# Degrees from a summed one-hot, two more groups multiplied in layer 0, fewer split feature sets: a two-layer graph kernel on one core

## What is computed

```python
deg = segment_sum(ones, dst); iso = deg == 0
def layer(h, edge_feats, Wn, Ws, Wi):
    msg = (h[src] + edge_feats) @ Wn.T
    agg = segment_sum(msg, dst) / maximum(deg, 1)[:, None]
    x = agg + where(iso[:, None], h @ Wi.T, h @ Ws.T)
    return where(x >= 0, x, SLOPE * x)
h = layer(x, edge_attr, Wn0, Ws0, Wi0)
h = layer(h, edge_attr, Wn1, Ws1, Wi1)
return layernorm(x + h)
```

## Time and profile before

| what | us |
|---|---|
| median of 3 runs | 1078.83 (1078.09 to 1083.72) |
| the profiled execution, its own time | 1072.14 |
| its span, first to last instruction | 1070.3 |
| windows of layer 0 on PE, about | 39 to 640 |
| windows of layer 1 on PE, about | 680 to 1058 |

### The profile page before, as it was taken

The page is one execution under the profiler, slowest core; times in us unless marked ns, Lnnn a source line. Parts: engine busy times, 40 slices in busy tenths (PEclk is TensorE's granted clock), DMA queues, the critical chain, the costliest instruction groups (busy, mean ns, idle before and its releaser), DMA issues.

```text
span 1070.3 us, 38440 instructions
## 1 busy us (share of the span) xinstructions
PE 942.5 (88%) x14592; PEld 880.3 (82%) x14592; DVE 696.6 (65%) x2388; ACT 534.1 (50%) x1143; POOL 756.2 (71%) x757
## 2 busy tenths in 40 slices
PE   1599899989899798998979987989899989999994
PEld 0499888978799687888878877989889989999994
DVE  8868776876778767887677782355455545554334
ACT  7456565655566555765656661353245525533200
POOL 8367767777777777777777671777767767767671
PEclk9999999999999989999999977999999999999998
DMA  9467777877788758877877777767656856676772
GB/s 306 158 214 248 256 252 240 264 259 233 244 283 277 255 169 268 285 241 255 261 220 230 242 243 241 238 172 218 177 157 171 236 157 168 170 222 168 206 217 60
DMA packets 141368, 237.75 MB, mean 222 GB/s; under 512 B 20050, under 2 KB 101308, under 8 KB 138620
## 3 DMA queue, kind: packets, MB, share of 16 engines
q1 hardware_dynamic: 80832, 144.35, 41.2%
q0 software_dynamic: 35584, 72.92, 25.1%
q10 hardware_dynamic: 24764, 17.95, 5.4%
HBM read 182.71 MB, written 52.43 MB: 220 GB/s over the span
## 4 chain that ended last, share of the span: by engine, by line
PE 45%; POOL 8%; issue 6%; DVE 4%; DMA 3%; ACT 3%; ACTq 2%; SPq 1%; DVEq 0%; POOLq 0%
PE ps_dense L1341 16%; PE ps_count L1341 11%; POOL rows L577 8%; PE ps_count L1329 6%; PE ps_win L1280 6%; PE ps_self L1399 3%; DMA rows<-x_parts_rows,idx 2%; ACT counts L1127 2%; PE ps_node L1412 2%; DMA h_parts<-h_parts_rows 1%; DVE h_rest L926 1%; SPq L498 1%; ACTq L1102 1%; PE ps_win L1287 1%; PE ps_count L1333 1%
## 5 line engine op out<-in xcount | busy, mean ns | idle before, releaser
L1127 ACT CAST counts<-ps_count 128x294 f32 x992 | 456.8, 502 | 346.0 <-PE ps_count L1329 207.4
L577 POOL DMA_INDIRECT rows<-x_parts_rows,idx x442 | 446.8, 1011 | 158.1 <-issue 125.0
L1341 PE MATMUL ps_dense<-counts,h_parts 128*128 128x136 bf16 x5292 | 450.3, 226 | 11.4 <-DVE sums L825 7.2
L1341 PEld LDWEIGHTS ps_dense<-counts,h_parts 128*128 128x128 bf16 x5292 | 350.6, 99 | 44.8 <-issue 9.2
L577 POOL DMA_INDIRECT rows<-h_parts_rows,idx x286 | 279.3, 977 | 127.6 <-issue 86.0
L1329 PE MATMUL ps_count<-is_code,is_lane 128*128 128x294 bf16 x992 | 285.5, 312 | 31.9 <-ACT counts L1127 27.2
L1280 PE MATMUL ps_win<-onehot,feats 128*128 128x40 f32 (+1 forms) x1564 | 253.4, 241 | 33.7 <-DMA rows<-x_parts_rows,idx 13.3
L1280 PEld LDWEIGHTS ps_win<-onehot,feats 128*128 128x128 f32 (+1 forms) x1564 | 212.7, 163 | 40.1 <-issue 25.5
L790 DVE TENSOR_SCALAR is_lane<-column,lane 128x128 bf16<-128x128 bf16 x496 | 138.4, 279 | 99.9 <-PE ps_count L1333 91.4
L792 DVE TENSOR_SCALAR is_code<-codes,code 128x637 bf16<-128x637 f16 x496 | 198.6, 400 | 0.0
L1280 PE MATMUL ps_win<-onehot,rows 128*128 128x40 bf16 (+1 forms) x2224 | 150.4, 187 | 2.3 <-DVE sums L803 2.3
(11 more groups left out here) (99 smaller groups left out, 790.6 us busy)
## 6 DMA issues: line engine op xcount, KB each, us to landing
feats<-in_edges_dram SPq DMA_DIRECT2D x196, 256.0 KB
counts_kept<-counts SPq DMA_DIRECT2D x20, 1764.0 KB
counts<-counts_kept SPq DMA_DIRECT2D x140, 252.0 KB
rows<-x_parts_rows,idx POOLq DMA_INDIRECT x442
x_parts_rows<-h_parts SPq DMA_DIRECT2D x7, 672.0 KB, 8.0
h_parts<-h_parts_rows SPq DMA_DIRECT2D x7, 672.0 KB, 8.7
h_parts_rows<-row_parts ACTq DMA_DIRECT2D x16, 288.0 KB
rows<-h_parts_rows,idx POOLq DMA_INDIRECT x286
```

The costliest lines, as they stand in the source:

```text
L577: nc.gpsimd.indirect_dma_start(rows[:, SUB * slot + c, :], None, table[:, :], bass.IndirectOffsetOnAxis(ap=indices[:, c:c + 1], axis=0)).t ...
L1127: nc.scalar.copy(counts[:, buffer_of(j), :, at(offset + first, count)], ps_count[:, COUNT_BANK[q], 0:count * TILES].rearrange("p (r t) -> ...
L1341: last = nc.tensor.matmul(bank, h_parts[:, t, k, :], counts[:, b, t, 0:WIDE], start=(t == 0 and k == 0), stop=(t == TILES - 1 and k == PAR ...
```

## The change

1. DVE gets one more step a window in layer 0, `sum_hot`: a reduction that adds the four one-hots (128x4x40, f32) to `hot_sum` (128x40). PE then makes one product with the ones instead of four. The step waits for the one-hot that it adds; PE waits for its result ahead of the last product of the window.
2. USED takes in groups 13 and 37: 22 groups are multiplied in layer 0, at 6.2 tiles a beat. LATE has 9 left. Eight windows are no longer gathered in layer 0. The number of builds (31 groups) and of groups multiplied in layer 1 stays; two groups are built in layer 0 and not in layer 1.
3. SPLIT_RATE is 0.3: 58 windows are split and not 78.

The beats of both layers stay 202 and 77.

```diff
-    USED = sorted([g for g in KEPT if g % 3 == 0] + [7, 19, 31, 43])
+    USED = sorted([g for g in KEPT if g % 3 == 0] + [7, 13, 19, 31, 37, 43])
-    BUILDS, MULTIPLIED, BUILT_BEAT, DONE_BEAT = plan_layer0(len(USED), 176, BUFFERS, GC, TILES, 5.6, 8)
+    BUILDS, MULTIPLIED, BUILT_BEAT, DONE_BEAT = plan_layer0(len(USED), 176, BUFFERS, GC, TILES, 6.2, 8)
-    SPLIT_RATE = 0.4
+    SPLIT_RATE = 0.3
+        hot_sum = sb("hot_sum", [P, HOT, W])
+            def sum_hot(n):
+                h = SUB * (n % HOT)
+                dve.wait_ge(onehot_ready, n + 1)
+                nc.vector.tensor_reduce(hot_sum[:, n % HOT, :],
+                                        onehot[:, h:h + SUB, :].rearrange("p c w -> p w c"),
+                                        AX.X, ALU.add).then_inc(hot_summed, 1)
                 for n in range(HOT):
                     make_onehot(n)
+                for n in range(HOT):
+                    sum_hot(n)
...
                     if k + 2 in SPLIT_OF:
                         split_feats(k + 2)
+                    if 1 <= k and k - 1 + HOT < WINDOWS:
+                        sum_hot(k - 1 + HOT)
...
                     if layer == 0:
-                        last = sum_degrees(ps_win[n % 2], onehot[:, SUB * (n % HOT):SUB * (n % HOT + 1), :], W, c + 1)
+                        pe.wait_ge(hot_summed, n + 1)
+                        last = nc.tensor.matmul(ps_win[n % 2][:, 0, DEG * W:(DEG + 1) * W], ones16[:, :],
+                                                upper(hot_sum[:, n % HOT, :]), start=True, stop=True)
                     last.then_inc(window_summed, 1)
```

More of the change, by code:

```diff
@@ L315, in gnn_resnorm_kernel @@
         onehot_ready = sem("onehot_ready")
+        hot_summed = sem("hot_summed")
         rows_gathered = [sem(f"rows_gathered{j}") for j in range(ROWS)]
```

## The result

The changed kernel takes 1083.79 us (median of 11 runs, 1079.75 to 1092.87) against 1078.09 us for the kernel before on the same chip (11 runs, 1073.14 to 1083.72). The ratio is 1.0054, 95% interval 1.0027 to 1.0080: slower by 5.7 us, where 1076 us was forecast, 3 us less than before.

A forecast was written before the change was run, and what follows sets the result against it. POOL and PE were taken as almost level in layer 0, PE as the bound of layer 1. Layer 0 at +5 and layer 1 at -6.6 us made -2, rounded to -3: 1076 us, range 1060 to 1094 (the forecast's own 1066 to 1084).

The forecast's parts named there:

- "up to 10 us" for fewer splits: POOL, layer 0: 20 fewer splits, less contention with DVE's subtractions, give POOL up to 10 us on top of 41.
- The prices on PE: PE, layer 0: prices per product, chunk and build taken from distances of starts; they sum to +18.9 us.
- the -6.6 forecast: Layer 1: PE loses 9.6 us of builds, one more restart waiting for ACT costs 3 us; -6.6 us.
- The load of the reduction: DVE, layer 0: 196 reductions at 0.33 us each, priced from two in setup, 65 us more on DVE.
- the 3 us in the sum for what DVE does late: Layer 0: PE's added waits for DVE's late adds of windows and groups, net of fewer last products; +3 us.
- 13.3 us of waits for rows: PE, layer 0: its waits for POOL's rows vanish because POOL has 41 us less work; -13.3 us.
- 5 us of clock: Layer 0: part of the lower granted clock comes back as the waits for rows go; about -5 us.
- Rival B: Layer 0, beats with a register load: DVE becomes the bound and its stops reach PE; +17, 1093 us; chance 0.24.
- Rival C: Layer 0: PE runs clean once rows are early, idle 36 us, half the clock loss back; 1062 us; chance 0.22.
- the terms of the sum: Both layers: PE's added products and builds against waits for rows, clock and layer 1; +9 us for parts 2 and 3.

The follow-up runs named there:

- no_deg_one: Kernel before with 22 groups and 58 splits, no reduction, and one column number loaded per beat instead of seven every seventh: 1049.89 us, ratio 0.9758.
- before_one: Kernel before with one column number loaded to a register in each beat instead of seven in every seventh: 1071.06 us, ratio 0.9957.
- all_but_deg: Kernel before with 22 groups and 58 splits but without the reduction (four products of degrees stay on PE): 1075.67 us, ratio 0.9991.
- deg_only_one: Kernel before with only the reduction added (20 groups, 78 splits) and one column number loaded per beat: 1080.93 us, ratio 1.0036.
- after_one: Changed kernel with one column number loaded in each beat of layer 0 instead of seven in every seventh: 1053.29 us, ratio 0.9788.
- pairs_one: Changed kernel with one addition in pairs and two products replacing the reduction and one product, and one column number loaded per beat: 1051.26 us, ratio 0.9750.
- after_early: Changed kernel with the load of seven column numbers moved to the end of the beat before: 1092.28 us, ratio 1.0128.

## Why the prediction was wrong

**POOL, right.** POOL was the bound of layer 0 and left it: PE's waits for rows went from 13.3 to 3.0 us, POOL's for PE from 20 to 79. `no_deg_one` against `before_one` shows that parts 2 and 3 are worth 21 us once PE can use the room. The "up to 10 us" for fewer splits was high: in the trace of before a gather that overlapped a subtraction took 1.07 us on average and another 0.98, about 3 us for 20 splits. That the reduction takes nothing from POOL holds: after the change, gathers beside it took 0.99 us and gathers beside neither 1.00.

**The prices on PE, right to within some 5 us.** PE's busy time in layer 0 rose by 20 us for 18.9 counted, but part of the rise is the lower clock of that one trace.

**Layer 1, right.** From its first to its last add of a window it is 371 us and was 379, for the -6.6 forecast. No waits for loads of counts came up.

**The load of the reduction, a size.** 0.33 us was taken from reductions of another shape; 0.43 us was measured, near the upper bound given. That is 19 us more on DVE. With its stops DVE was 91% taken (505 busy and 45 stopped of 605 us), for 90% forecast.

**The step that failed** is the 3 us in the sum for what DVE does late, and with it the two gains that it left standing in full, 13.3 us of waits for rows and 5 us of clock. PE's waits for the adds of windows rose by 10.0 us and those for groups by 0.8, 10.8 us and not 3. They took the place of the 10.3 us of waits for rows that went: PE's idle time stayed at 54 us, and the clock, which was to rise with less idling, did not (0.956 over the runs). The forecast was 8.7 us below the median of the change (-3 against +5.7); the waits are 8 us of it and the clock 5, and terms that came out better, layer 1 for one, give some back.

The mechanism behind the 3 us was wrong too. They were sized as half of PE's waits for adds and a tenth of those for groups, as if lateness grew with the load of DVE. `all_but_deg` has no reduction, and PE waits for the adds as long as in the changed kernel. What reaches PE in these two kernels is the single long load. (Load alone can make the adds late too: `deg_only_one` has no long load, and PE waits 13.2 us for them.) The rows held the warning: 28.2 us in 18 stops, the longest 4.6 us, was read as an average of 1.6 us. With two banks at about three us a beat, loads of up to 2.5 us never reached PE in the changed kernel and those of 3.2 us and more always did. `after_one` shows the size: taking away the long loads, with more time spent on loads in all, is worth 30 us with the reduction, 26 without (`all_but_deg` to `no_deg_one`), and 6 with 20 groups and no reduction.

**Rival B** named the right place, the beats with a register load, with a chance of 0.24, and the right sign; the 1093 that it gave was too high. Its account was not right: it made the reduction the cause, by the slack that it takes from DVE, and that slack (77.5 us in `all_but_deg`, 32 in the changed kernel) made no difference to the waits for adds. **Rival C**, PE running clean once rows are early, is what was left when the long loads went: in `after_one` PE is idle 36 us in layer 0, as C had it, at a clock of 0.97, and the time is 1053 for its 1062.

For parts 2 and 3 alone the terms of the sum give 33.6 - 13.3 - 5 - 6.6 = +9 us. They measured nothing with loads of seven and -21 us with single ones. In the second pair idle time fell by 24 us (49 to 25) and the clock in layer 0 rose from 0.95 to 0.98: together more than twice the 18 us that the sum had for them.

The Trainium skill (VectorE: DVE Perf Modes, Rules for kernel authors) calls `tensor_reduce` the slowest DVE op and advises considering a restructuring on a hot path. The traces agree: 0.43 us, against 0.24 us for the addition in pairs. With single loads that made 2 us in the time, less than can be told apart (`after_one` against `pairs_one`), so what it is worth depends on what else holds the kernel up.

**Still open**: whether the stores of counts cause the long loads and whether moving them would do what single loads did; how much of the rise in PE's waits for adds came of more long loads and how much of POOL no longer being in front; why the clock is lower with part 1 and in `after_early`; and whether another layout of the one-hots would shorten the reduction.

## What to carry to other kernels

When a change takes the bound off one engine, look for the longest single stop on the engines that the next one depends on, not for their busy share or for the average stop: in the changed kernel two banks hid every load up to 2.5 us and none from 3.2 us on. Register loads are in no busy time; look up their line, look at what the DMA engines do at the long ones, and spread such loads one a step rather than batching them, if the trace shows that single ones are short. Do not book a wait that a change removes as a gain before asking which wait was hidden behind it; the same goes for the clock that was to come back with it. A product saved on the bound engine can cost more than it saves: the same reduction cost 22, 10, 7 and 3 us, depending on what else held the kernel up.

## What the runs showed of the hardware

A register load of one number on DVE took 0.31 us at the median (196 loads in `after_one`, 297 ns to 1.6 us); loads in layer 1, of one or four numbers, mostly 0.35 us; a load of seven from neighbouring places 1.0 us at best, 1.6 to 1.8 at the median and up to 6.4 us. Beside a store of 1764 KB by the DMA engines they took longer: seven numbers 4.0 us on average and 1.5 elsewhere (changed kernel), one number 0.78 and 0.34 (`after_one`). Seven single loads (2.2 us) are no shorter than one median load of seven, but DVE's add was held up by 10.6 us in all and not 45.4.

A tensor_reduce of 128x160 f32 with strided reads took 428 ns, and the addition of two halves of the same inputs by a tensor_tensor (128x80) 239 ns.
